# Routing a transformer layer's last batch in two halves, with the last two attention heads interleaved and empty expert slots skipped

## What is computed

```python
a = (q @ k.T * scale) ** 2 * exp(logG_t - logG_s)   # causal
y = (a @ v) / (a.sum(-1) + 1e-6)                    # per head
x = layernorm(x + y @ Wc + bc)
scores = softmax(x @ gate_w.T); topk_w, topk_idx = top_k(scores, 6)
# every expert: its rows, silu(x@g)*(x@u) @ down, weighted, added to its tokens
x = layernorm(x + experts(x) + shared_swiglu(x))
```

## Time and profile before

| what | value |
|---|---|
| median of three runs | 2573.97 us (2572.37 to 2574.27) |
| the profiled execution | 2557.7 us |
| span in it, first to last instruction | 2555.9 us |
| PE / DVE / ACT / POOL busy | 2312.3 / 1397.8 / 1248.9 / 1578.3 us |
| mean granted clock of TensorE | 0.96 |
| bytes moved by DMA | 329.68 MB |
| last attention matmul ends at about | 1757.7 us |
| first expert transposes at about | 1927.8 us |
| last add of expert rows landed at about | 2515 us |

### The profile page before, as it was taken

One profiled execution on the slowest core, in us unless ns is written; L12 is line 12 of the kernel. 1 busy time (PEld: TensorE's weight loads), 2 busy tenths in 40 slices (PEclk: granted clock), 3 DMA queues, 4 the chain that ended last, 5 costly groups with the idle time before them and its releaser, 6 DMA issues.

```text
span 2555.9 us, 34620 instructions
## 1 busy us (share of the span) xinstructions
PE 2312.3 (90%) x11876; PEld 1793.6 (70%) x11880; DVE 1397.8 (55%) x2813; ACT 1248.9 (49%) x2302; POOL 1578.3 (62%) x1421
## 2 busy tenths in 40 slices
PE   5999999999999899999999999998797999989981
PEld 4777776776767677776667777666685887778871
DVE  2444444445564454557445455745666766656664
ACT  3444444444434344343444443434234777767764
POOL 2566555544578654457855445784074888788885
PEclk8999999999999999999999999999798999999996
DMA  3766741122123112111411211224355999889987
GB/s 125 302 238 261 279 157 63 54 63 64 40 64 119 54 52 87 40 40 69 138 31 53 88 40 38 71 76 146 119 188 163 216 212 202 193 197 213 210 165 230
DMA packets 162663, 329.68 MB, mean 129 GB/s; under 512 B 17552, under 2 KB 98192, under 8 KB 162480
## 3 DMA queue, kind: packets, MB, share of 16 engines
q1 hardware_dynamic: 114144, 262.01, 30.4%
q0 software_dynamic: 48192, 65.04, 14.0%
q10 hardware_dynamic: 144, 0.33, 0.0%
HBM read 172.21 MB, written 155.11 MB: 128 GB/s over the span
## 4 chain that ended last, share of the span: by engine, by line
PE 61%; POOL 10%; DMA 9%; DVE 8%; issue 7%; ACT 5%; POOLq 0%; SPq 0%; ACTq 0%; DVEq 0%
PE bank L686 37%; PE bank L1038 13%; POOL slots L1944 4%; DMA y_part<-y_e,xr 4%; PE bank L696 4%; POOL nacc L1903 3%; PE bank L1048 3%; DMA xr<-slots 3%; POOL y_part L1954 2%; PE bank L1138 2%; PE bank L1035 1%; DVE acc L1563 1%; DMA w_raw_f<-in_wffn,job_w 1%; ACT a L1288 1%; DVE ub L1526 1%
## 5 line engine op out<-in xcount | busy, mean ns | idle before, releaser
L1903 POOL TENSOR_TENSOR nacc<-nacc,a 128x512 f32<-128x512 f32 (+1 forms) x384 | 448.0, 1167 | 286.7 <-ACT a L1292 137.6
L1038 PE MATMUL bank<-a,v 128*128 128x512 f32 x1024 | 529.3, 598 | 0.0
L1954 POOL DMA_INDIRECT y_part<-y_e,xr x256 | 436.5, 1705 | 119.2 <-issue 74.5
L1288 ACT ACTIVATE a<-bank,c_s 128x512 f32<-128x512 f32 x384 | 263.7, 687 | 164.2 <-PE bank L686 148.5
L686 PE MATMUL bank<-q_hi,k_hi 128*128 128x512 f32 (+1 forms) x640 | 324.4, 507 | 12.1 <-DVE ub L1526 6.0
L1292 ACT ACTIVATE a<-ub 128x512 f32<-128x512 f32 (+1 forms) x256 | 133.9, 523 | 394.5 <-DVE ub L1526 382.9
L1903 POOL TENSOR_TENSOR nacc<-a,a 128x512 f32<-128x512 f32 (+1 forms) x128 | 148.9, 1163 | 252.1 <-ACT a L1288 194.6
L1944 POOL DMA_INDIRECT slots<-rows,slot_u x192 | 198.3, 1033 | 163.0 <-DVE slot_u L1689 110.9
L1563 DVE SCALAR_TENSOR_TENSOR acc<-bank,rec,acc 128x256 f32<-128x256 f32 x512 | 223.3, 477 | 98.5 <-PE bank L686 94.5
L686 PE MATMUL bank<-q_lo,k_hi 128*128 128x512 f32 (+1 forms) x640 | 240.0, 375 | 0.0
L686 PE MATMUL bank<-q_hi,k_lo 128*128 128x512 f32 (+1 forms) x640 | 238.3, 372 | 0.0
(11 more groups left out here) (212 smaller groups left out, 5671.6 us busy)
## 6 DMA issues: line engine op xcount, KB each, us to landing
slots<-acc SPq DMA_DIRECT2D x65, 816.0 KB, 7.2
w_raw_f<-in_wffn SPq DMA_DIRECT2D x66, 624.0 KB, 6.7
xr<-slots SPq DMA_DIRECT2D x64, 544.0 KB, 4.6
decay_all<-decay_dram SPq DMA_DIRECT2D x128, 128.0 KB, 3.4
w_hi<-w_dram SPq DMA_DIRECT2D x24, 384.0 KB, 4.7
w_lo<-w_dram SPq DMA_DIRECT2D x24, 384.0 KB, 5.4
sum<-y_part SPq DMA_DIRECT2D x16, 512.0 KB, 10.7
wc_hi<-wc_dram SPq DMA_DIRECT2D x24, 256.0 KB, 3.9
```

Source lines behind the costliest of these rows:

```text
L1038: e.matmul(dst, v[n % 3][:, s, :], a32[u % NA][:, :, :], start=first, stop=False, skip_group_check=True).then_inc(s_av)
L1288: e.activation(squares, score_bank(u)[:, 0:R * w].rearrange("p (r t) -> p r t", r=R), ACT.Square, scale=c_s[b % 2][:, g * (g - 1) + s, h:h ...
L1903: e.tensor_tensor(out_, a, b, op).then_inc(s_nadd)
L1954: e.indirect_dma_start(out=y_part[part], out_offset=bass.IndirectOffsetOnAxis(ap=x_rows[:, j, TOKEN_COL:TOKEN_COL + 1].bitcast(U32), axis= ...
```

## The change

1. **Order of the last two heads.** The units of heads 30 and 31 (offsets 0 to 39) are put in one list by hand, so that both heads' queries 0 to 511 are done by offset 15. The loads, masks and decays get places by hand, and head 31's six `col` tasks stand at offsets -3, -2, -1, 4, 9 and 13. The number of units and tasks is the same.
2. **The last batch's routing in halves.** `PARTS` has five parts: batches 0 to 2 and two halves of batch 3, 27 steps and 24 scatters each. The first half's steps begin behind offset 19, one per unit; 20 of them run in attention, 7 behind `gate_up(0)`. The second half's 27 steps are spread over k = 1 to 11 by a list of paces. In the last two heads a scatter piece of batch 2 is issued at every unit and not at every second one.
3. **The sum.** The normed rows are stored straight into `y_part[1]`; `x1_dram`, its loads for the shared expert and DVE's addition are gone, and ACT copies the result of `shared_down`.
4. **Empty slots.** Their token number becomes 2^20, beyond the bounds check of the adding DMA, which now leaves such rows out; the spare rows of `y_part` and 8 of 73 `fill` DMAs are gone.
5. `rows_in(0)` and `rows_in(1)` stand ahead of the last `shared_out` in SP's list. Some waits become exact (`read_until`, `place_free`).

```diff
+LAST = HEADS - 2
+LAST_UNITS = (before(LAST, 1) + diagonal(LAST, 0) + diagonal(LAST, 1) + diagonal(LAST + 1, 0) + before(LAST + 1, 1)
+              + before(LAST, 2) + diagonal(LAST + 1, 1) + before(LAST, 3) + diagonal(LAST, 2) + diagonal(LAST, 3)
+              + before(LAST + 1, 2) + before(LAST + 1, 3) + diagonal(LAST + 1, 2) + diagonal(LAST + 1, 3))
+UNITS_ALL = [(n, g, s) for n in range(LAST) for g, s in UNITS] + LAST_UNITS
...
+PARTS = [(b_, 0, TILES) for b_ in range(B - 1)] + [(B - 1, t_, TILES // 2) for t_ in (0, TILES // 2)]
...
+def route_steps(p):
+
+    pairs = range(PARTS[p][2] // 2)
+    steps = ([f"stat{j}" for j in pairs] + ["std"] + [f"norm{j}" for j in pairs] + ["store"]
+             + [f"{what}{k}" for k in pairs for what in ("x1t", "logit")] + ["softmax0", "softmax1", "max", "index"]
+             + [f"{what}{q}" for q in pairs for what in ("hot", "chosen")] + ["chosen_bf", "weight0", "weight1", "count", "slots"]
+             + [f"{what}{q}" for q in pairs for what in ("again", "send")])
+    return [(p, step) for step in steps]
...
+    cols_at = {-3: (1, 0, 0), -2: (0, 0, 0), -1: (0, 1, 0), 4: (1, 0, 1), 9: (0, 0, 1), 13: (0, 1, 1)}
+    first_half_routed_at = 19
...
+            step_from = u + (2 if p < B - 1 else 1)
...
-        if to_send and at in send_at:
+        if to_send and (at in send_at or n >= LAST):
             do(*to_send.pop(0))
...
             do("gate_up", 2 * m + half)
+            route_some(paces[2 * m + half])
             hidden(2 * m + half)
...
+    paces = [len(background) - 27, 4, 2, 1, 2, 2, 2, 3, 3, 2, 4, 2]
...
             on_spare("shared_down", m, pair)
+        if m == M - 1:
+            do("rows_in", 0)
+            do("rows_in", 1)
...
+        read_until[n, 1, s * P // 512] = read_until[n, 0, g * GROUP // 512] = u
...
+    def place_free(n, g):
+
+        return GROUP_NTH[n - 1, g] + 1 if n else 0
...
-                e.dma_start(xr[r][:, :, 0:C], x1_dram[ms, :].rearrange("(j p) c -> p j c", p=P)).then_inc(c_r[r], 16)
...
+                e.dma_start(y_part[1][first_row(p):first_row(p) + PARTS[p][2] * P, :].rearrange("(j p) c -> p j c", p=P),
+                                rows[:, tiles_in(p), 0:C]).then_inc(s_x1_out[p // B], 16)
...
+                e.activation(y_e[y][:, js, :], bank[6 + m % 2][:, :].rearrange("p (j c) -> p j c", c=C), ACT.Copy).then_inc(s_out_of[m % 2])
...
-                    in_=y_e[y][:, j, :], in_offset=None, bounds_check=N + CAP - 1, oob_is_err=True,
+                    in_=y_e[y][:, j, :], in_offset=None, bounds_check=N - 1, oob_is_err=False,
...
-            e.iota(slot0[:, :, TOKEN_COL].bitcast(I32), pattern=[[P, CT]], base=N, channel_multiplier=1).then_inc(s_init)
+            e.iota(slot0[:, :, TOKEN_COL].bitcast(I32), pattern=[[P, CT]], base=NOWHERE, channel_multiplier=1).then_inc(s_init)
```

More of the change, by code:

```diff
@@ L82, with before, diagonal @@
 NU = len(UNITS)
[L83 to L94, removed]
+def before(n, g):
+    return [(n, g, s) for s in range(2 * g)]
+def diagonal(n, g):
+    return [(n, g, 2 * g), (n, g, 2 * g + 1)]
+LAST = HEADS - 2
[3 more added lines that the diff above has]
+UNITS_ALL = [(n, g, s) for n in range(LAST) for g, s in UNITS] + LAST_UNITS
+GROUPS = [(n, g) for n, g, s in UNITS_ALL if s == 2 * g + 1]
+GROUP_NTH = {group: i for i, group in enumerate(GROUPS)}
+NA, NS = 7, 2
+PARTS = [(b_, 0, TILES) for b_ in range(B - 1)] + [(B - 1, t_, TILES // 2) for t_ in (0, TILES // 2)]
[6 more added lines that the diff above has]
+    return [(p, step) for step in steps]
+SENDS = 6
 def f32(ap):
@@ L229, in schedule @@
         do("score", u)
-    for u, (n, g, s) in enumerate(UNITS_ALL):
-        at = u % NU
+    for u, (n_, g, s) in enumerate(UNITS_ALL):
+        n, at = divmod(u, NU)
         catch_up()
[L233 to L239, removed]
+        if at == 0 and n < LAST:
+            if (n + 1) % H == 0:
+                must += gate_tasks((n + 1) // H)
+            must += qkv_tasks(n + 1)
+            first = 2 if (n + 1) % H == 0 else 0
+            must_at = [first + i * (NU - ahead - first) // len(must) for i in range(len(must))]
         if u + ahead < len(UNITS_ALL):
-            if UNITS_ALL[u + ahead][0] != n:
+            if (u + ahead) // NU != n:
                 while must:
@@ L316, in schedule @@
     catch_up()
[L317 to L320 removed]
+    background += route_steps(B)
     def route_some(count):
+        while to_send:
+            do(*to_send.pop(0))
         for _ in range(min(count, len(background))):
[L324 removed]
+            route_step(*background.pop(0))
             while to_send:
@@ L362, in schedule @@
             do("split_lo", m - 2)
-    route_some(len(background))
+    assert not background and not to_send
     do("counted",)
@@ L572, in build @@
             a32 = [sb(att, f"a32_{i}", [P, R, GROUP]) for i in range(NA)]
-            nacc = [sb(att, f"nacc{i}", [P, R, GROUP]) for i in range(NJ)]
+            nacc = [sb(att, f"nacc{i}", [P, R, GROUP]) for i in range(NG)]
             nrm = sb(att, "nrm", [P, 2 * R])
@@ L727, in rows_wait @@
                 once.wait_ge(c_add[prev % 2], added(prev))
-            else:
-                last = max(m for m in range(M) if m % XS == x_id % XS)
-                once.wait_ge(*out_of(("shared_down", last, 1)))
         def y_wait(once, x_id):
@@ L1047, in norm @@
                         k = tt * R + r
-                        ins = e.matmul(av_bank(j)[:, k:k + 1], nacc[j % NJ][:, r, tt * P:(tt + 1) * P], ones[:, 0:1], start=(k == 0),
+                        ins = e.matmul(av_bank(g)[:, k:k + 1], nacc[g][:, r, tt * P:(tt + 1) * P], ones[:, 0:1], start=(k == 0),
                                        stop=True, skip_group_check=True)
@@ L1265, in col @@
                 if n >= 2:
-                    once.wait_ge(s_scores, (n - 1) * NU)
+                    once.wait_ge(s_scores, read_until[n - 2, which, tc] + 1)
                 e.activation(dst, bank[6 + m % 2][:, :], ACT.Copy).then_inc(s_split_hi)
@@ L1581, in route @@
                     steps_done()
-                    for j in range(TILES):
+                    for j in each:
                         ins = e.bn_aggr(mv[:, j, :], stats[:, j, :])
@@ L1676, in route @@
                     steps_done()
-                    step(e.tensor_tensor(slot_of[:, :, :], slot_of[:, :, :], over[:, :, :], ALU.add))
+                    step(e.tensor_tensor(slot_of[:, ts, :], slot_of[:, ts, :], over[:, ts, :], ALU.add))
                 elif name[:4] == "send":
-                    q = int(name[4:])
-                    js = slice(q * q4, (q + 1) * q4)
+                    j0 = t0 + int(name[4:]) * QT
+                    js = slice(j0, j0 + QT)
                     steps_done()
-                    for jj in range(q4):
+                    for jj in range(QT):
```

381 lines of the change are left out of this document (199 added, 182 removed).

## The result

The changed kernel takes 2544.31 us (median of four runs, 2541.57 to 2548.16), the kernel before, in the runs beside it, 2574.12: ratio 0.9892 [0.9877, 0.9907], 29.8 us less. The forecast was 2546 us, from -28.

A forecast was written before the change was run, and what follows sets the result against it. The prediction took the middle stage to be bound by routing on DVE and PE, then 48 scatters on POOL, then two transfers. Its terms -29 + 13 - 12 = -28 us took 2574 to 2546 us, range 2520 to 2565.

The forecast's parts named there:

- Part 1: Between attention and experts: routing the last batch in halves takes 24 scatters off the chain, experts start earlier; -29 us.
- their cover: Middle stage: 16 copies of 0.6 us cost nothing on ScalarE, busy 50 of 170 us; otherwise 1.2 us more per block.
- Part 2: Last two heads of attention: reordering, front-loaded scatters and moved routing work make attention end later; +13 us.
- PE would thus stand for about 15 us behind `norm`: Last two heads: before `norm(31, 1)` POOL needs 54 us of work, PE 39 us for its units and `col` tasks.
- DVE gets 8 routing steps into units in which it is busy 40.7 of 93.2 us: End of attention: DVE's spare half covers the steps at no cost; without that cover, up to 15 us.
- Part 3: Experts' flow: leaving out empty slots removes a quarter of the adds, so landings and PE's waits for rows shrink; -12 us.
- The loop of five buffers needs only some 2 us less: Experts' flow: some 2 us less in the buffer loop would let it fit five experts, easing PE's waits for rows.
- The constant: Whole kernel: the profiled execution lies 16.3 us below the median of three runs, kept unchanged in the forecast.
- The backlog does not stop PE: Rival, chance 0.20: tiles and scores ahead absorb POOL's scatter backlog, attention ends as before; 2533 us.
- The relief is not felt: Rival, chance 0.15: fewer adds bring the experts nothing, through latency, POOL's pace or descriptors still used; 2558 us.
- Felt whole: Rival, chance 0.12: with fewer adds PE never waits in the experts' flow, -27 us there; 2531 us.
- The slower one: Rival, chance 0.05: skipped rows make each expert's four adds cost POOL 2.08 instead of 1.56 us; 2658 us.

The follow-up runs named there:

- r3: The changed kernel, unedited, run and profiled again on another chip; 2529.57 us, ratio 0.9907 to the kernel before.
- r2: The kernel before the change, unedited, run and profiled again on another chip; 2554.19 us, ratio 1.0.
- e2: The changed kernel with no routing step of batch 3 inside attention, all behind `gate_up(0)`, order of heads kept; 2544.25 us, ratio 0.9962.
- e7: The changed kernel with only the first ten of 20 routing steps inside attention, the other ten after `gate_up(0)`; 2543.06 us, ratio 0.9871.
- r1: The changed kernel, unedited, run and profiled again on another chip; 2546.06 us, ratio 0.9888.
- e4: The kernel before with nothing changed but the empty slots left out of the adding DMAs; 2549.59 us, ratio 0.9970.
- e5: The changed kernel with the empty slots added again to spare rows, with two more fills; 2553.47 us, ratio 0.9915.
- e6: The changed kernel with batch 2's scatters evenly spaced, routing steps of both halves respread around the shared expert, and a load moved; 2536.18 us, ratio 0.9844.
- e1: The changed kernel with batch 2's scatter pieces back at every second unit in the last two heads, plus two places; 2532.56 us, ratio 0.9919.

## Why the prediction was right, point by point

**Total.** -28 was forecast, -29.8, -29.5 and -23.8 were measured on chips A, C and D. In the clean pair, r3 against r2, the stages give +14.2 - 30.0 - 4.6 - 0.1 = -20.5 us for the -29 + 13 - 12 of the sum; their medians differ by 24.6 us. The nearness on A and C is in part luck: the changed kernel loses 10 us or more to stops there, which no term has, and the kernel before is 20 us slower there than on D, for which no trace gives the reason.

**Part 1, -29: right, and as it was worked out.** -30.0 on chip D. The second half's first scatter was to start at 1859 + 13 = 1872 us, the first transposes near 1912. POOL's timeline in r3, then a stretch of that kernel's chain, and PE's waits from 1775 to 1928 us:

```profile
1793.66 1.01 POOL L2002 DMA_INDIRECT slots<-rows,slot_u  x1 [20.12 <-DVE slot_u L1758]
...
1825.49 0.98 POOL L2002 DMA_INDIRECT slots<-rows,slot_u  x1 [0.30 <-issue]
...
1872.17 0.99 POOL L2002 DMA_INDIRECT slots<-rows,slot_u  x1 [45.53 <-DVE slot_u L1758]
...
1904.77 1.00 POOL L2002 DMA_INDIRECT slots<-rows,slot_u  x1 [0.30 <-issue]
```

```profile
1892.00 8.33 PE bank L758 x36
1900.33 9.60 PE bank L768 x80
```

```profile
PE bank L758 <- DVE h_b L1775: 12.2, 4, 6.5
PE bank L758 <- DMA xe_lo<-x1t_dram: 10.0, 1, 10.0
PE bank L1202 <- DMA xr<-slots: 1.2, 1, 1.2
```

24 scatters from 1793.7 us (forecast 1787, so 7 us late and without effect), 24 from 1872.2, spaced (1904.77 - 1872.17)/23 = 1.42 us. PE's own shared work ends at 1909.9 us and it waits 1.2 us for the rows: the two chains are level, as worked out. PE waits 12.2 us for `hidden`'s `h_b`, where the working had some 12 us of idle time ahead of `gate_up(2)` and `(3)`. PE waited 0.2 us for ScalarE's copies of the shared result, so their cover held. On chips A and C the middle stage is 10.7 and 12.8 us longer, which takes the first transposes to 1925.0 and 1925.5 us. The prediction counted a start after 1925 us as proof against it; by its own test it stood on the line on A and just past it on C. The same kernel starts them at 1911.1 us on D, 1 us from the forecast.

**Part 2, +13: the size right, what it is made of wrong.** +14.2 on D, +16.1 on A. The step that failed is "PE would thus stand for about 15 us behind `norm`". In r3 that `norm` starts at 1716.1 us (1721 in the working), after a wait of 5.8 us: POOL was ready 5 us earlier, and PE came 4 us later, than worked out. The kernel before has such a wait of 4.9 us (r2), so it grew by 0.9 us. e2, without a routing step, waits 5.9 us at the same place. With the scatters out early, POOL is then free again: in r3 it is idle for 3.2, 4.5 and 2.6 us at a time between 1730 and 1751 us.

What came in its place are the routing steps. From the start of that `norm` to the end of attention the units are the same in e2 (no step), e7 (ten) and r3 (twenty):

```profile
1716.67:1759.94 43.27, 43.13 (x201) 31.65 (x201) 18.10 (x43) 17.13 (x33) 31.59 (x32) 0.95 0.03 7
1716.63:1766.42 49.79, 47.62 (x233) 34.83 (x233) 23.41 (x61) 20.93 (x38) 31.70 (x33) 0.95 0.12 38
1716.09:1770.60 54.51, 50.62 (x233) 37.03 (x233) 33.33 (x88) 21.23 (x39) 32.34 (x33) 0.91 0.11 35
```

The first ten steps add 32 matmuls and 4.5 us of PE's busy time, which the sum has as 4 us, and 2.0 us of idle time. The last ten add no matmul, yet PE is busy 3.0 us longer, with the granted clock at 0.91 instead of 0.95, and idle 1.7 us longer. r1, on e7's chip, has the same 54.5 us as r3, with 50.6 busy and a clock of 0.91. So the steps cost 11.2 us, and the other 3.0 of the 14.2 come before that `norm`; e2 has them too, among them a wait of 2.7 us for DVE's `nrm`. The sentence "DVE gets 8 routing steps into units in which it is busy 40.7 of 93.2 us", costed at nothing, was the error: 20 steps ran there, and an average share of DVE was taken for cover. A step of 1.4 us ahead of a masked tile delays it even if DVE is idle for half of the stage. That I came out near is luck: a wait that did not grow stood for idle time and slower matmuls that the sum does not have.

**Part 3, -12: too large.** The experts are 12.3 us shorter on A, but 4.6 on D, and skipping alone is worth 6.7 us (e4) and 7.4 (e5). What differed was the kernel before: PE waited 25.2 us for rows in the profile that I read the earlier trace rows, 17.7 in r2; in the changed kernel's three traces it is 13.0, 12.6 and 12.4. The term was taken from one execution with unusually many waits. Waits, queues and landings of r3, from 1960 to 2450 us:

```profile
PE bank L1202 <- DMA xr<-slots: 12.4, 9, 2.8
PE bank L768 <- ACT y_e L1430: 3.6, 2, 3.2
```

```profile
q1 hardware_dynamic: 16272, 67.54, 41.9%
q0 software_dynamic: 34531, 25.21, 38.7%
xr<-slots SPq DMA_DIRECT2D x57, 544.0 KB, 4.2
y_part<-y_e,xr POOLq DMA_INDIRECT x236, 5.1
```

The queue's share fell to 38.7 points for a forecast of 37, so skipped rows do save their transfers, which was open. An add lands in 5.1 instead of 5.3 us. By the Trainium skill, page "DMA: Bandwidth & Descriptors", section on the anatomy of one DMA, the saving is an estimated 0.08 us of a landing. In the single landing the trace nearly agrees (0.1 to 0.2 us). That rule would give the kernel almost nothing, and there the runs disagree: 256 adds gave about 7 us. In pairs from one chip the waits for the rows fell by 5.3 us (r2 to r3) and 3.9 us (e5 to r1), and in r3 PE waits 3.6 us for ScalarE's `y_e`, which r2 does not. But the waits are no sure measure: kernels that skip have 10.7 (e6) to 19.5 us (e1) of them, and e5 and r2, which do not, 16.5 and 17.7. Where the 7 us lie is therefore only in part shown. The loop of buffers did not become free, contrary to "The loop of five buffers needs only some 2 us less". The time on POOL did not change, as taken; two adds of the changed kernel (chip A), its median over 256 being 1.55 us:

```profile
2004.92 2.12 POOL L2012 DMA_INDIRECT y_part<-y_e,xr  x1 [0.30 <-issue]
2007.35 1.55 POOL L2012 DMA_INDIRECT y_part<-y_e,xr  x1 [0.31 <-issue]
```

**The constant.** The 16.3 us between profile and median were kept as a constant. They are not one: on chip A it is 2.8 us for the changed kernel (2541.57 against 2544.31). So the first pair of profiles shows 16.2 us and the medians 29.8. What the other 13 us are is open; the first profile of the kernel before may not be from chip A at all, as said above.

**The rivals.** "The backlog does not stop PE" was nearly right in its mechanism (5.8 us of waiting for 4.9 before) and wrong in its number (2533): attention ended late all the same. "The relief is not felt" falls by e4 and e5. "Felt whole" falls by the 12 to 13 us of waits that stay in the changed kernel. The slower one falls by the adds above.

## What to carry to other kernels

Work that is moved beside a stage whose engines are each "half idle" is not free. Ask for each moved instruction what stands behind it in its engine's queue: its length is what the next thing that the bound engine needs can lose. Here twenty steps cost 11 us, of which 4.5 were the matmuls that had been counted. Shortening a serial chain pays most where a part of it runs under other work: here 10 us for the halves with what came along, and 20 more for the half that was moved, against the 11 to 14 us that it cost in attention. A term taken from the waits of one execution can be off by as much as executions differ: 25.2 us of waits in one trace of the kernel before, 17.7 in the next. And compare variants only on one chip: e1 looked 10 us better in the middle stage than the changed kernel, and beside it was 5 us slower.

## What the runs showed of the hardware that was not expected

In the traces of A and C, and not in those of B and D, PE stops for 0.2 to 2.3 us at a time within otherwise dense work, and ScalarE and DVE with it (ScalarE for 3.6 us once on A), with no semaphore or transfer that the profile could name. In two traces of the same kernel (A and r1) the stops are at nearly the same places (`shared_down(0)` near 1816, the last two near 1911 to 1917 us). The granted clock falls behind them (0.76 for 1.00), and the middle stage grows by 10.7 and 12.8 us. What the engines wait for was not found: there was no experiment that changes it by itself.

Routing steps without a matmul made matmuls slower. In the stretches shown in part 2 the granted clock is 0.95 with PE idle for 0.1 us (e2) or 2.2 us (e7), and 0.91 with PE idle for 3.9 us (r3 and r1), where the same 233 matmuls as in e7 take 3.0 us longer. That the idle time lowers the clock is an inference from these traces; no run changes it alone.

Adding DMAs of which a quarter of the rows is left out by the bounds check take as long on POOL as full ones (1.55 for 1.56 us). The queue gives back by bytes and not by landing time: on chip D 31.67 MB became 25.21 (20% less) and its share 49.0 points became 38.7 (21% less), while an add landed 0.2 us sooner.
